# Layer 0's routing and its experts in one block: gate and up products beside the routing, logits in the norm

## The reference, cut to what matters

```
scores = sigmoid(x @ gate_w.T)                       # (T, 64)
choice = scores + gate_bias
group_scores = sum of the top 2 of choice in each of 8 groups of 8
masked = choice where the group is among the top 4 groups, else 0
topk_idx = the top 8 of masked
topk_w = 2.5 * scores[topk_idx] / (sum + 1e-20)
rw = topk_w scattered back to (T, 64)
mlp(x, g, u, d) = (silu(x @ g.T) * (x @ u.T)) @ d.T
out = sum over 64 experts of mlp(x, Wg, Wu, Wd) * rw[:, e]  +  mlp(x, Sg, Su, Sd)
x = layernorm(x + out)
```

## Time and profile before

| | us |
|---|---|
| median of 3 runs | 1408.93 |
| lowest and highest | 1405.17, 1409.25 |
| the profiled execution | 1402.02 |
| its span, first to last instruction | 1400.3 |
| mean granted TensorE clock | 0.946 of full speed |

### The profile page before, as it was taken

One profiled execution on the slowest core, in us unless ns is written; L12 is line 12 of the kernel. 1 busy time (PEld: TensorE's weight loads), 2 busy tenths in 40 slices (PEclk: granted clock), 3 DMA queues, 4 the chain that ended last, 5 costly groups with the idle time before them and its releaser, 6 DMA issues. The chain is left out here.

```text
span 1400.3 us, 21389 instructions
## 1 busy us (share of the span) xinstructions
PE 1279.3 (91%) x7374; PEld 711.9 (51%) x7374; DVE 1114.2 (80%) x1726; ACT 898.5 (64%) x1503; POOL 481.3 (34%) x988
## 2 busy tenths in 40 slices
PE   5898987169999999999889999999999998999998
PEld 2222224157777777777643232223222337777776
DVE  5677763758999999999758788888889747688886
ACT  4988873034555555555453788888888866767775
POOL 4565551014334343334142244224422422221210
PEclk8898988579999999999999999999999999999999
DMA  5422200064666666666236555434342201121200
GB/s 156 127 56 66 63 21 7 0 134 110 147 143 154 148 151 151 147 146 152 79 113 146 111 156 133 121 102 104 88 123 61 53 11 52 62 91 46 91 31 31
DMA packets 70020, 135.87 MB, mean 97 GB/s; under 512 B 13031, under 2 KB 44328, under 8 KB 63112
## 3 DMA queue, kind: packets, MB, share of 16 engines
q1 hardware_dynamic: 68760, 133.46, 37.5%
q10 hardware_dynamic: 1152, 1.05, 0.2%
HBM read 116.87 MB, written 16.29 MB: 95 GB/s over the span
## 5 line engine op out<-in xcount | busy, mean ns | idle before, releaser
L1589 ACT ACTIVATE a_PR<-n1a_C 128x512 f32<-128x512 f32 x576 | 299.6, 603 | 79.5 <-PE n1a_C L1495 79.4
L1604 DVE CUSTOM_DVE_ANT_0 OC_last<-a_mring,a_COR 128x1024 bf16<-128x1024 f32 x256 | 302.6, 1218 | 42.4 <-PE a_mring L1462 42.1
L1432 POOL TENSOR_SCALAR_AFFINE_SELECT a_PR<-a_PR 128x128 f32<-128x128 f32 x512 | 136.2, 296 | 250.2 <-ACT a_PR L1589 249.7
L868 ACT ACTIVATE e_HH<-e_H 128x512 fp32r<-128x512 f32 x184 | 116.4, 633 | 158.3 <-DVE e_H L916 157.5
L1495 PE MATMUL n1a_C<-a_QP,a_KP 74*128 74x512 bf16 (+3 forms) x768 | 176.1, 332 | 4.4 <-ACT a_PR L1589 3.5
L402 ACT ACTIVATE a_PR<-a_ring,a_ng 128x1024 f32<-128x1024 f32 (+1 forms) x160 | 150.2, 1045 | 26.0 <-PE a_ring L345 26.0
L427 DVE TENSOR_SCALAR a_PR<-a_PR,a_lo,a_hi 128x1024 f32<-128x1024 f32 (+1 forms) x160 | 119.2, 763 | 56.1 <-ACT a_PR L402 55.6
L1514 PE MATMUL n1a_C<-a_PR,a_V 128*9 128x512 f32 (+3 forms) x1536 | 152.1, 492 | 0.0
L887 DVE TENSOR_TENSOR e_HL<-e_H,e_HH 128x512 fp32r<-128x512 f32 x138 | 139.4, 1010 | 13.5 <-DVE e_H L904 0.5
L810 POOL TENSOR_TENSOR e_HL<-e_H,e_HH 128x512 fp32r<-128x512 f32 x46 | 78.5, 1706 | 180.5 <-ACT e_HH L868 180.5
L1883 DVE TENSOR_TENSOR e_HL<-e_GL,e_HH 128x512 fp32r<-128x512 f32 x144 | 109.5, 765 | 38.3 <-ACT e_HH L1851 34.7
(11 more groups left out here) (257 smaller groups left out, 2252.6 us busy)
## 6 DMA issues: line engine op xcount, KB each, us to landing
e_ROUTE<-routing SPq DMA_DIRECT2D x24, 704.0 KB
a_QP<-q_parts SPq DMA_DIRECT2D x72, 192.0 KB
e_RAW<-in_w_chunks SPq DMA_DIRECT2D x46, 192.0 KB, 7.4
a_QM<-q_parts SPq DMA_DIRECT2D x64, 128.0 KB, 2.8
e_GATE<-gates SPq DMA_DIRECT2D x8, 1024.0 KB, 4.4
e_ROUTE<-routing SPq DMA_DIRECT2D x8, 640.0 KB
a_KP<-k_parts SPq DMA_DIRECT2D x24, 192.0 KB
e_ROUTE<-routing SPq DMA_DIRECT2D x8, 576.0 KB
```

The source lines that it names most:

```text
L868: nc.scalar.activation(HH[n % NH][:], HT[n % NH][:], ACT.Copy).then_inc(high_done, 1)
L1432: last = nc.gpsimd.affine_select(out=d, in_=d, compare_op=keep, fill=0.0, base=0, pattern=[[step, P]], channel_multiplier=-step)
L1589: nc.scalar.activation(PR[:, g % NPR, j, :], ring[n % NRING][:], ACT.Exp).then_inc(s_read, 1)
L1604: nc.vector.tensor_tensor_reduce(out=junk[:, i % 2, :], in0=mring[k % 2][:], in1=COR[:, c:c + S], scale=1.0, scalar=-3.0e38, op0=ALU.mult, ...
```

## The change

One block, `moe_l0`, takes the place of `route_l0` and `experts_l0`, and part of the work moves ahead into the norm's block (class `AheadMoeL0`).

- **In the norm's block**: SyncE loads the router's operands and the first four chunks' RAW; GpSimd splits three chunks; PE makes the logits of each token group behind its rescaling; ScalarE makes X's high part and the four sigmoids, GpSimd X's low part.
- **Routing chain on VectorE**: shorter (the top 2 of a group by maxima and minima of halves; ties by one comparison), and 20 products stand in it.
- **PE**: gate and up products for tiles 0 to 19, the shared expert's down products by one plain fp32 matmul a tile (L828 of the new file), then the turning of the ratios, which waits for `weights_ready`, in the four banks of psG and psU. ScalarE copies the ratios, SyncE stores them.
- **Lag**: weighing and high run 20 tiles behind the product (`BEHIND`), the down product 23 behind (`DOWN`). T has 24 buffers and is weighed in place.
- **Buffers**: RAW 4 (`NRAW`), split weights 8 (`NSLOT`), ROUTE 2 (`NR`) in place of 3.
- **SyncE's order**: RAW(c) once split(c-4) is done, then ROUTE(c-9) once chunk c-11 is weighed. **GpSimd's order**: split(c), low(4(c-6)+3), split(c+1), and so on. For the last 20 tiles GpSimd also makes the lows of every second tile of a chunk.
- `OC`, `WOT`, `WOC` and the like are one tensor for both layers; Y is written to OC.
- **Layer 1's projection**: PE's wait for `cor_loaded` moves from the last group to the one before it, with 5 `keep_busy` added there; the 16 at the end are 5.

The core of the diff:

```diff
@@ normalise: PE @@
                     variance_of(g)
                     spread_inverse(g - 1)
+                    if ahead is not None and g >= 2:
+                        ahead.logits_of(pe, g - 2, done, base + g - 1, C[g - 2])
                 spread_inverse(NG - 1)
+                if ahead is not None:
+                    for g in range(NG - 2, NG):
+                        ahead.logits_of(pe, g, done, base + g + 1, C[g])
@@ AheadMoeL0 @@
+    def load_chunk(self, sp, c):
+        if c >= NRAW:
+            sp.wait_ge(self.w_split, 2 * (c - NRAW + 1))
+        if NRAW <= c < NRAW + CHS:
+            sp.wait_ge(self.down_done, (c - NRAW + 1) * NG)
+        sp.dma_start(self.RAW[c % NRAW][:], self.a["w_chunks"][c]).then_inc(self.w_loaded[c % NRAW], 16)
+    def split(self, pool, c):
+        raw, high, low = self.RAW[c % NRAW], self.WH[c % NSLOT], self.WL[c % NSLOT]
+        pool.wait_ge(self.w_loaded[c % NRAW], (c // NRAW + 1) * 16)
+        if c >= NSLOT:
+            pool.wait_ge(self.down_done, (c - NSLOT + 1) * NG)
@@ moe_l0: SyncE @@
+                def load_route(c):
+                    if c >= CHS + NR:
+                        sp.wait_ge(h_ready, (c - NR - CHS + 1) * NG)
...
-                for c in range(NW, NCH):
-                    sp.wait_ge(w_split[c % NW], c // NW * 2)
-                    load(c)
-                    if c >= CHS + NW:
-                        sp.wait_ge(h_ready, (c - NW + 1) * NG)
-                        load_route(c)
+                for c in range(2 * NRAW, NCH):
+                    ahead.load_chunk(sp, c)
+                    if c - 2 * NRAW - 1 >= CHS + NR:
+                        load_route(c - 2 * NRAW - 1)
+                for c in range(NCH - 2 * NRAW - 1, NCH):
+                    load_route(c)
@@ moe_l0: GpSimd @@
+                for c in range(ahead.FIRST, NCH + POOL_BEHIND):
+                    if c < NCH:
+                        ahead.split(pool, c)
+                    if c - POOL_BEHIND >= CHS:
+                        for n in range((c - POOL_BEHIND) * NG, (c - POOL_BEHIND + 1) * NG):
+                            if on_pool(n):
+                                low(n)
@@ moe_l0: TensorE @@
+                    if n == TURN:
+                        turn_weights()
...
+                    if 3 <= n < NSH + 3:
+                        down_shared(n - 3)
+                    if n - DOWN >= NSH:
+                        down(n - DOWN)
@@ moe_l0: VectorE, behind the chain @@
+                for n in range(products[0], BEHIND + NSH):
+                    product(n)
+                for n in range(BEHIND + NSH, N + BEHIND + 1):
+                    if n < N:
+                        product(n)
+                    if n - BEHIND - 1 >= NSH:
+                        low(n - BEHIND - 1)
+                    if n - BEHIND < N:
+                        weigh(n - BEHIND)
@@ project_l1 @@
-                        pe.wait_ge(cor_loaded, 32)
...
+                    if g == NG - 2:
+                        pe.wait_ge(cor_loaded, 32)
+                        keep_busy(psV, 5)
...
-                keep_busy(psQ[0], 16)
+                keep_busy(psQ[0], 5)
```

More of the change, by code:

```diff
@@ L521, in _ @@
                     nc.scalar.activation(dev_of[:, g], scale[g][:, 0:TG], ACT.Sqrt, bias=consts["eps"][:]).then_inc(dev, 1)
+                    if ahead is not None and g >= 2:
+                        ahead.high_of_x(act, g - 2, done, base + g - 1)
+                if ahead is not None:
+                    for g in range(NG - 2, NG):
+                        ahead.high_of_x(act, g, done, base + g + 1)
+                    for g in range(NG):
+                        ahead.scores_of(act, g, C[g])
+            if ahead is not None:
+                @block.gpsimd
+                def _(pool):
+                    for c in range(ahead.FIRST):
+                        ahead.split(pool, c)
+                    for g in range(NG):
+                        ahead.low_of_x(pool, g)
             @block.vector
@@ L727, in experts_l0, with moe_l0 @@
+def moe_l0(nc, X, Y, last_outputs, ahead, consts, routing, part):
+    NR = 2
     NH = 4
-    LAG = 3
+    TURN = 20
+    BEHIND = 20
+    DOWN = BEHIND + 3
+    NTR = 24
     NSH = CHS * NG
@@ L731, in experts_l0 @@
     N = NCH * NG
-    ON_POOL = (3,)
+    POOL_BEHIND = 6
     def segments(c):
@@ new lines, in link @@
+                def link(ins, then=0):
+                    links[0] += 1
+                    ins.then_inc(step, 1)
+                    for _ in range(then):
+                        product(products[0])
+                        products[0] += 1
+                    dve.wait_ge(step, links[0])
+                by_group = ch.rearrange("p t (g e) -> p (t g) e", g=NGRP)
+                flat = lambda t: t[:].rearrange("p t g -> p (t g)")
+                wide = lambda t, k: flat(t).unsqueeze(2).to_broadcast([P, NT_TOK * NGRP, k])
@@ new lines, in _ @@
+                upper = t1.rearrange("p t e -> p (t e)")[:, 0:NT_TOK * NE0 // 2].rearrange("p (g e) -> p g e", e=GSZ // 2)
+                lower = t1.rearrange("p t e -> p (t e)")[:, NT_TOK * NE0 // 2:].rearrange("p (g e) -> p g e", e=GSZ // 2)
+                quarter = lambda n: t2.rearrange("p t e -> p (t e)")[:, n * NT_TOK * NE0 // 4:(n + 1) * NT_TOK * NE0 // 4]\
+                    .rearrange("p (g e) -> p g e", e=GSZ // 4)
+                first, other, third = quarter(0), quarter(1), quarter(2)
```

409 lines of the change are left out of this document (195 added, 214 removed).

## The result

The changed kernel takes 1454.65 us (median of 3 runs, 1449.99 to 1456.04), the kernel before 1408.93: ratio 1.0325, 95% interval 1.028 to 1.037. It is slower, as forecast, by 45.7 us where 21.4 were forecast, and lies 0.65 us above the upper end of the range. The three runs themselves lie 6 us apart, so those 0.65 us mean nothing; the change that is over twice the forecast is what has to be explained. The profiled execution of the changed kernel has a span of 1448.0 us (before 1400.3). A second series of the same kernel, on another occasion, gave 1454.36 and a ratio of 1.0339 (1.029 to 1.039).

The account below looks back on a forecast made before the run. VectorE, held up by GpSimd, was taken to set the loop's pace, with PE close behind. Y's end at 716.7 for 691.8 us, less 3.5 in layer 1, gave +21.4 and a median of 1430.3; range 1382 to 1454.

Parts of the forecast that it names:

- the line: Loop: ROUTE's issue waits behind RAW, split, low and high after the weighing that frees its buffer; 19.6 us for two chunks.
- A: Norm's block: logits and sigmoids made there let the routing chain start at 245.9 us and not at 252.56.
- B: Routing chain on VectorE with 20 products in it: 47 us, ratios ready at 292.9 where they were at 283.66.
- C: From the chain's end to the first weighing: ratios' store, landing and ROUTE, 15.5 us, so 308.4 where it was 314.16.
- D: Expert loop, chunk 2 to 36: queued work delays ROUTE, 9.7 us a chunk (9.1 to 10.2), 329.8 us; the deciding term.
- E: Chunk 36 to the end of Y: 78.5 us, ending at 716.7 where it was 691.80.
- F: Layer 1 behind Y: fewer filling matmuls and a better clock gain 3.5 us (-1 to 6).
- the third rival: Products don't fit under the chain: PE at half clock, 70 us in place of 47, 1453 us; chance 0.10.
- The first two rivals: Loop: ratios in time, pace 8.37, median 1385, chance 0.20; or shorter line, 9.1 to 9.2 a chunk, 1412, chance 0.14.
- the signs that the prediction named: Loop: weighings wait 2 to 5 us for ROUTE, SyncE issues RAW then ROUTE behind GpSimd's subtraction, PE's share 85%.
- the first rival: Loop: ratios arrive in time, transfers up to 5.3 us cost nothing, pace 8.37, median 1385; chance 0.20.
- a slow stretch in the attention: Layer 1: if the shorter filling at the end brings a slow stretch into the attention, 4 us lost.

Follow-up runs that it names:

- ROUTE first: Changed kernel with one swap in SyncE's order: the loads of ROUTE(r) ahead of the load of RAW(r+9); 1391.6 us, ratio 0.9888.
- changed kernel, undone filling: Changed kernel with layer 1's filling as it was (16 at the end, none in the third group); 1456.8 us, ratio 1.0355.
- all three, undone filling: The kernel of all three with layer 1's filling matmuls as they were; 1385.3 us, ratio 0.9874.
- before, new filling: The kernel before with only the changed filling of layer 1's projection (5 at the end, 5 in the third group); 1404.2 us, ratio 0.9991.
- third buffer: Changed kernel with three ROUTE buffers for two (NR = 3) and nothing else; 1447.9 us, ratio 1.0289.
- split first: Changed kernel with GpSimd's split of chunk r+5 ahead of the low of chunk r-2's last tile (POOL_BEHIND = 7); 1390.3 us, ratio 0.9873.
- half of ROUTE: Changed kernel loading only 1024 of ROUTE's 2048 columns from the third routed chunk on, same order; 1393.6 us, ratio 0.9909.
- all three: Changed kernel with ROUTE's loads ahead of RAW's, GpSimd's split ahead of the low, and three ROUTE buffers together; 1388.0 us, ratio 0.9863.
- RAW early: The kernel of all three with RAW(8) and RAW(9) issued ahead of the ratios' store; 1379.0 us, ratio 0.981.

## Why the prediction was right and wrong

The direction and the mechanism were right: the line through the queues sets the pace, and the weighings wait for ROUTE. What failed is the size. In the deciding term the 8.2 us for RAW's and ROUTE's transfers were 9.0, and the term for layer 1, a gain of 3.5 us, was a loss of 5.4 that changes from one execution to the next. By its steps, in the frame of the profiled executions:

| | predicted | measured | after |
|---|---|---|---|
| A, chain starts | 245.9 | 244.95 | |
| B, length of the chain | 47 | 42.25 | ends 287.2 |
| C, to the first weighing | 15.5 | 19.3 | 306.48 |
| D, chunk 2 to 36 | 329.8 | 346.6 | 653.10 |
| E, to the end of Y | 78.5 | 81.0 | 734.12 |
| F, the rest (708.5 before) | 705.0 | 713.9, 708.3 the second time | |

Term by term the miss in this frame is 26.3 us: D 16.8, F 8.9, C 3.8, E 2.5, less 4.8 of B and 0.9 of A.

**A** was right within 1 us, in part by luck: the attention ahead of it, which the change does not touch, ends at different times. In the ten profiles of changed kernels the last rescaling started between 240.7 and 247.1 us, in the two of the kernel before (one with the new filling) at 239.3 and 246.9. What does not vary is the distance: the chain starts 4.25 us behind the last rescaling's start in all ten, 13.3 in the two.

**B** was 4.8 us too long. VectorE's groups within the chain:

```profile
L910 DVE TENSOR_TENSOR e_T<-e_SG,e_psU 128x512 f32<-128x512 f32 x20 | 13.7, 684 | 4.0 <-PE e_psU L821 4.0
...
L947 DVE TENSOR_TENSOR OC<-r_scores,r_bias 128x1024 f32<-128x1024 f32 x1 | 1.5, 1489 | 3.6 <-PEq L462 3.6
...
L949 DVE TENSOR_TENSOR OC<-OC 128x512 f32<-128x512 f32 x1 | 1.4, 1378 | 0.0
```

The 20 products cost 13.7 us, for 13.6 predicted. They waited 4.0 us for PE, for 5 predicted, and the clock was near half only at the start (0.52 from 244 to 250 us, 0.92 in the next 6). GpSimd's block was 0.26 + 0.70 us on two instructions (1.49 for 1.23, 1.38 for 0.68), for 2 predicted. The chain by itself, 42.25 - 13.7 - 4.0 - 0.96 = 23.6, was 3 us shorter than my 26.5: I had priced its many small instructions too high, or kept the 2.0 us for which VectorE stood idle in the old chain and which products now fill. The two are not told apart. So the third rival, that the products do not fit, did not come about.

**C** was 3.8 us too short. In SyncE's and VectorE's timelines the ratios' store was issued from 288.97 to 291.97 (4.8 us behind the chain's end, 4.9 predicted), its landing took until 295.33 (3.4, for 2 predicted), and ROUTE, issued then with the next chunk's loads right behind it, was there at 306.48: 11.2 us, for 8 predicted.

```profile
288.97 3.00 SPq L789 DMA_DIRECT2D routing<-r_RT  x4
295.33 1.53 SPq L782 DMA_DIRECT2D e_ROUTE<-routing  x4
296.90 22.27 SPq L668 DMA_DIRECT2D e_RAW<-in_w_chunks  x6
```

B and C cancel, and the first weighing came at 306.48 for 308.4.

**D** was the term that decides, and its mechanism is shown: the swap alone, the split alone and the bytes alone each move the pace as the line says, and the buffer alone does not. Its size was 17 us too small, 10.19 a chunk for 9.7. Link by link, the mean of 29 lines between 316 and 600 us against the prediction:

| link | predicted | measured |
|---|---|---|
| four weighings | 7.74 | 7.30 |
| high | 0.74 | 0.74 |
| low, cast, subtraction | 2.93 | 3.15 |
| to RAW's issue | | 0.03 |
| RAW's issue to the weighing | 8.2 | 9.01 |
| two chunks | 19.6 | 20.2 |

In 22 of the 29 lines the weighing waited for ROUTE, and the last link is 8.99 in these.

The step that failed in D is the 8.2 us for RAW's and ROUTE's transfers: 0.81 us too short in two chunks, 13.8 of the 16.8 us over 34 steps. It was taken from RAW's landing in the kernel before, where RAW stands behind ROUTE; I took that for the landing of both. ROUTE's own could not be read there, since nothing waited for it. Where a weighing does wait, it shows, and the waits fall in two groups, by how a ROUTE is cut into loads. In the changed kernel up to chunk 36, the 18 waited ROUTEs that have a load of 88 rows (704 KB) took 8.6 to 10.0 us from their first issue to the weighing; of the 8 whose loads have at most 80 rows, seven took 7.3 to 7.7 us, and the eighth, with the next ROUTE's loads right behind it, 9.5. One of each group, with two loads both, chunk 23's (40 and 88 rows; issued at 512.17 and used at 521.27, above) and chunk 25's (48 and 80):

```profile
532.39 0.89 SPq L782 DMA_DIRECT2D e_ROUTE<-routing  x2
```

```profile
539.67 0.69 DVE L918 TENSOR_TENSOR e_T<-e_T,e_ROUTE 128x512 f32<-128x512 f32 x1 [1.97 <-DMA e_ROUTE<-routing]
```

9.10 and 7.28 us. With the 0.40 us from RAW's issue to ROUTE's, the 8.2 was right for the second group and 1 to 2 us short for the first. The 13 waiting weighings of the loop with ROUTE first, where RAW is not in the way, start 8.6 to 9.3 us behind ROUTE's first issue, and all 13 are of the first group. So the time goes with how a ROUTE is cut. No run changed the cut: that the 88 rows are the cause is read off these rows and not shown, and why they would be is open.

My choice within the bounds, 9.7 where the measured rows gave 9.8, was sound. I had argued that fewer lows are blocked when VectorE waits. In part they are: the four weighings took 7.30 for 7.74. In part the block moves to GpSimd, whose low and cast took 1.60 and 0.96 us on the first weighings of a pair's second chunk, where they had been 1.28 and 0.50. With the measured links and my 8.2 the sum is 19.4, just 9.7 a chunk. The rest of D's miss, some 3 us, lies outside these lines, at the loop's start. The first two rivals (8.4 and 9.2 a chunk) did not come about. Of the signs that the prediction named, the waits for ROUTE (0.2 to 6.5 us), SyncE's two issues right behind a subtraction and PE's share (88% for 85%) came.

The page's rule that stands beside the first rival, by which a load of 1 MB would land 4.4 us behind its issue (the Trainium skill, DMA: Bandwidth & Descriptors, section Anatomy of one DMA (SWDGE path)), is given for one DMA that GpSimd issues, and does not hold for these loads, two or three to a ROUTE and issued by SyncE: the runs show 7.3 to 10.0 us for a whole ROUTE in the changed kernel, and 5.6 us from RAW's issue with half of it.

**E** was 2.5 us too short. The four last steps, for which 6.8 us each were predicted, took 6.6, 8.8, 5.8 and 8.8, and at the end of both long ones a weighing waited 2.4 and 2.5 us for ROUTE. The five chunks ahead of them, 38.9 us, took 1.1 less than predicted, and the last one with the additions 0.6 more.

**F** had the wrong sign: 3.5 us gained predicted, 5.4 lost in the profile. The step that failed is that it was priced from one execution at all. The rest of the program behind Y, which is the same code but for the filling, took these times:

| profile | filling | rest, us |
|---|---|---|
| before | old | 708.5 |
| changed kernel, undone filling | old | 717.6 |
| all three, undone filling | old | 709.7 |
| before, new filling | new | 710.1 |
| changed kernel | new | 713.9 |
| changed kernel, again | new | 708.3 |
| third buffer | new | 713.8 |
| ROUTE first | new | 709.3 |
| split first | new | 711.5 |
| half of ROUTE | new | 708.7 |
| all three | new | 716.8 |
| RAW early | new | 716.6 |

Both kinds span nearly the same 9 us. What the filling is worth is not to be seen under that, and the timed runs show nothing that their intervals can tell (0.25% to either side for the kernel before, 3.5 us). It also means that the 47.7 us between the two profiled spans are not all the change's: with the second profile of the changed kernel they are 41.1, and 5.6 of the 6.6 us between those two lie behind Y.

**The range** ended at 1454.0. It took the 10.2 of D in, but for F only 1 us of loss. With the 5 us of spread in F added, as the prediction's own sentence on a slow stretch in the attention ("4 us lost") asked, it would have held the result. That is a remark on the range alone: its middle was off by D's 16.8 us first.

**What the change is worth without the line.** The head is really shorter: from the start of the norm's last rescaling to the first weighing it is 64.2 to 65.9 us in the ten profiles of changed kernels and 74.9 and 75.9 in the two of the kernel before. With ROUTE first the whole kernel is 15.7 us faster than before, with all queues in order 26. The blind forecast of the direction came from one thing: reading for each load what stands ahead of it in its queue and what that waits for.

## What to carry to other kernels

When loads of several kinds share one issue queue, write down for each what stands ahead of it and what that waits for, through the other engines' queues too; a load whose buffer is free early can be held up by one whose buffer is not, and a third buffer does nothing against that, while one swap in the order costs nothing. Put the load with the tightest buffer first. Take a transfer's time from an instruction that waited for it, not from the landing of its neighbour; and take a stretch whose granted clock differs between two executions as a spread, not as a term of the sum.

## What was unexpected in the hardware

- A ROUTE (1 MB in two or three broadcasts from DRAM) took 8.6 to 10.0 us to the instruction that waited for it when one of its loads had 88 rows, and 7.3 to 7.7 in seven of the eight cases in which none had over 80, the same bytes in all. Only ROUTEs that were waited for can be timed so. A RAW load (192 KB) ahead of it lands in 2.5 us, behind it in 7.2.
- The same program spent 20 us of layer 1 at a granted clock of 0.57 in one execution and of 0.91 in another, and the stage behind Y took 713.9 and 708.3 us. PE was busy for 19.2 and 17.2 of those 20 us.
- VectorE loses to GpSimd 1.07 us a chunk or 0.3 us, by where in its queue GpSimd's work falls: 8.26 us a chunk in the kernel with RAW early, 8.16 in all_three, with the same instructions in the loop.
